# Attention of a transformer layer on one core: the order of the work rebuilt around pairs of heads and pairs of query tiles

## What is computed

```python
x = x + attn(layernorm(x))    # 16 heads, 64 plain + 64 rotated dims each, causal
x = x + ffn(layernorm(x))     # ternary weights: sign(W) * mean|W|, SiLU gate, 2048 wide
# attn, per head h:
scores = q[h] @ k[h].T * 128 ** -0.5          # causal, k from x, q from a latent of 256
out   += softmax(scores) @ (kv_lat @ Wv_up[h]) @ Wo[h]   # kv_lat: latent of 128
```

## Time and profile before

| | us |
|---|---|
| median of 3 runs | 2064.77 |
| lowest, highest | 2064.74, 2067.74 |
| the profiled execution | 2071.07 |
| its span, first to last instruction | 2069.3 |
| PE busy | 1929.1 (93%) |
| DVE busy | 1350.7 (65%) |
| ACT busy | 1060.1 (51%) |
| POOL busy | 526.0 (25%) |

### The profile page before, as it was taken

The page is one execution under the profiler, slowest core; times in us unless marked ns, Lnnn a source line. Parts: engine busy times, 40 slices in busy tenths (PEclk is TensorE's granted clock), DMA queues, the critical chain, the costliest instruction groups (busy, mean ns, idle before and its releaser), DMA issues. The chain is left out here.

```text
span 2069.3 us, 31835 instructions
## 1 busy us (share of the span) xinstructions
PE 1929.1 (93%) x11304; PEld 1668.5 (81%) x11304; DVE 1350.7 (65%) x2832; ACT 1060.1 (51%) x2531; POOL 526.0 (25%) x333
## 2 busy tenths in 40 slices
PE   6888875799999999999999999999999979999999
PEld 4666664699898898899899899889989968787877
DVE  5455554678778788788788688788778763333333
ACT  2233332567566566576566576576666652222222
POOL 6234343523222331331331322422412100000000
PEclk9998988899999999999999999999999989999999
DMA  3497988721120320320310301302202030000000
GB/s 109 137 232 206 228 203 215 205 62 27 53 62 1 78 62 1 79 60 3 78 38 26 78 15 48 78 1 62 68 11 62 1 123 1 21 0 20 0 20 20
DMA packets 67594, 144.61 MB, mean 70 GB/s; under 512 B 6880, under 2 KB 23520, under 8 KB 63328
## 3 DMA queue, kind: packets, MB, share of 16 engines
q1 hardware_dynamic: 67424, 142.50, 26.1%
HBM read 94.24 MB, written 48.23 MB: 69 GB/s over the span
## 5 line engine op out<-in xcount | busy, mean ns | idle before, releaser
L996 ACT CAST turned_hi<-ps_turn 128x512 fp32r<-128x512 f32 (+1 forms) x576 | 314.4, 566 | 377.2 <-PE ps_turn L1164 377.2
L1070 DVE TENSOR_TENSOR turned_lo<-ps_turn,turned_hi 128x512 fp32r<-128x512 f32 (+1 forms) x576 | 370.1, 659 | 129.1 <-ACT turned_hi L996 124.6
L969 ACT ACTIVATE probs<-ps_scores,bias 128x512 f32<-128x512 f32 (+3 forms) x642 | 401.6, 634 | 27.6 <-DVE bias L1063 12.9
L1164 PE MATMUL ps_turn<-ident,probs 128*128 128x128 f32 x2176 | 319.1, 275 | 0.8 <-ACT probs L969 0.2
L1134 PE MATMUL ps_scores<-k_hi,q_hi 128*128 128x512 f32 (+2 forms) x642 | 258.8, 403 | 37.0 <-issue 24.4
L1164 PEld LDWEIGHTS ps_turn<-ident,probs 128*128 128x128 f32 x2176 | 250.8, 140 | 27.1 <-ACT probs L969 3.0
L1037 DVE TENSOR_REDUCE negmax<-ps_scores 128x1 f32<-128x512 f32 x384 | 258.4, 681 | 3.5 <-PE ps_scores L1134 3.3
L1141 PE MATMUL ps_o<-turned_hi,kv_hi 128*128 128x256 f32 x1152 | 248.0, 297 | 6.2 <-DVEq L1069 6.1
L1134 PE MATMUL ps_scores<-k_lo,q_hi 128*128 128x512 f32 (+2 forms) x642 | 239.3, 373 | 0.0
L1134 PE MATMUL ps_scores<-k_hi,q_lo 128*128 128x512 f32 (+2 forms) x642 | 238.0, 371 | 0.0
L1141 PEld LDWEIGHTS ps_o<-turned_hi,kv_hi 128*128 128x128 f32 x1152 | 199.7, 190 | 44.4 <-issue 11.5
(11 more groups left out here) (156 smaller groups left out, 3495.6 us busy)
## 6 DMA issues: line engine op xcount, KB each, us to landing
rotT<-rot_out SPq DMA_DIRECT2D x64, 256.0 KB, 4.3
plainT<-plain_out SPq DMA_DIRECT2D x64, 256.0 KB, 5.1
k_raw<-plainT SPq DMA_DIRECT2D x16, 512.0 KB, 5.5
k_raw<-rotT SPq DMA_DIRECT2D x32, 256.0 KB, 6.6
q_raw<-plainT SPq DMA_DIRECT2D x16, 512.0 KB, 8.5
q_raw<-rotT SPq DMA_DIRECT2D x32, 256.0 KB, 9.0
all_signs<-signs SPq DMA_DIRECT2D x24, 256.0 KB, 4.8
signs_in<-all_signs SPq DMA_DIRECT2D x12, 512.0 KB, 8.7
```

The costliest lines, as they stand in the source:

```text
L969: nc.scalar.activation(probs[:, u % 2, t, first_key:first_key + keys], ps_scores[:, n % RING, 0:keys], ACT.Exp, scale=-1.0 if crosses(u, t ...
L996: nc.scalar.copy(turned_part(0, n, u, s), turned_psum(n, u, s)).then_inc(turned_hi_ready, 1)
L1070: nc.vector.tensor_tensor(turned_part(1, n, u, s), turned_psum(n, u, s), turned_part(0, n, u, s).bitcast(F32), ALU.subtract).then_inc(turn ...
L1164: last = nc.tensor.transpose(ps_turn[:, n % 2, at * P:(at + 1) * P], probs[:, u % 2, t, key:key + P], ident[:])
```

## The change

Only `attention` and its plan are rewritten. Both heads of a pair are worked on together: a tile of 128 queries has both heads' columns side by side.

- *Tiles and slots.* `SLOTS` pairs tile 15 with 0, 14 with 1, and so on to 8 with 7: 8 slots a pair, each with 9 steps and 10 pieces of scores over both heads. The first tile of a pair is thus the one with the most keys.
- *Steps.* A step is up to two key blocks of one tile, both heads: four transposes, or two where one block is left (`step_blocks`). No block above the diagonal is turned or multiplied: three value matmuls of 256 columns a block.
- *Two steps together.* `turn` of an even and the following odd step stand side by side in the plan, two steps ahead of their values; both banks of `ps_turn` are taken at once (`TURN_BANKS`), the turned halves have four places (`TURNED`). All values of a step wait for `turned_lo`.
- *Outputs.* Four a slot (two tiles, two heads), all in the second bank of `ps_o`, which also holds the values of the slot's second tile. Each waits for the add before it.
- *The plan.* `Plan` gives every event a time in steps (72 a pair) and sorts by it. Scores stand one slot ahead of the turns, across pairs: an event whose time falls before or after the pair's 72 steps belongs to the body of the pair before (`EARLY`) or after (`LATE`). Every pair's body is written out with those of its neighbours: one before the loop, 3 iterations of two pairs each, one behind it.
- *Loads.* k comes in four chunks of 512 tokens, both heads (`load_k`, 3 DMAs), q by slot (`load_q`, 6 DMAs of 128 tokens), wvo by head (`load_w`). `k_raw` and `q_raw` have two places each, `w_raw` one; each load waits until GpSimd has split what was there. The splits stay 18 a pair, each 512 columns.
- *Start.* No load is issued before the stores have left. Then the first pair's `EARLY` part runs: k chunks 0 and 1, wvo, k chunk 2, wvo, k chunk 3, q of slots 0 to 2, and behind them a sign chunk and `y`. VectorE waits for all of `y` between that part and the first pair's own.

TensorE's order by plan time in slot 1 (steps 9 to 17), from step 10: turn 3 and 4; scores; scores; out; scores; values 1; values 2; out; turn 5 and 6; out; values 3; scores; scores; out; values 4; scores; scores; turn 7 and the first of the second tile; values 5; values 6; scores; turn, turn; values 7; scores; values. In VectorE's order from the same turn: turned_lo 3, maximum, add, maximum, maximum, turned_lo 4, add, turned_lo 5, add, maximum, turned_lo 6, maximum, add, maximum, maximum, turned_lo 7, turned_lo. In ScalarE's: turned_hi 3, turned_hi 4, exp, split, exp, turned_hi 5, exp, turned_hi 6, exp, split, turned_hi 7, turned_hi, exp, exp, exp, exp, split, turned_hi, turned_hi.

The diff, cut to the plan, the loops of SP and VectorE, and TensorE's body:

```diff
--- before.py
+++ after.py
-QCH = 256
-TPU = QCH // P
-UPH = T // QCH
-UNITS = 2 * UPH
 PIECE = CH
 RING = 4
-SPLITS = 2 * NC + 1
-FIRST = 3
...
+TURN_BANKS = 2
+TURNED = 4
+RAW = 2
+SLOTS = tuple((NT - 1 - n, n) for n in range(NT // 2))
+NSLOTS = len(SLOTS)
+def npieces(t):
+    return -(-(t + 1) // TC)
+def piece(t, p):
+    return p * PIECE, min(PIECE, (t + 1) * P - p * PIECE)
+def nsteps(t):
+    return -(-(t + 1) // 2)
+def step_blocks(t, s):
+    return min(2, t + 1 - 2 * s)
+class Plan:
+    SCORES = {(4, 1): (0.5, 1.2, 1.6, 1.7, 3.8, 3.9, 4.6, 4.7, 6.7, 8.2),
+              (3, 2): (0.0, 0.8, 0.9, 1.5, 2.7, 3.6, 5.0, 5.2, 5.5, 6.7)}
+    def __init__(self):
+        self.events = []
+        lengths = [sum(nsteps(t) for t in tiles) for tiles in SLOTS]
+        begin = [sum(lengths[:n]) for n in range(NSLOTS)]
+        self.total = sum(lengths)
+        step = 0
+        for n, tiles in enumerate(SLOTS):
+            at = iter(self.SCORES[tuple(npieces(t) for t in tiles)])
+            for i, t in enumerate(tiles):
+                for h in range(2):
+                    for p in range(npieces(t)):
+                        x = begin[n] - lengths[n - 1] + next(at)
+                        self.put(x, "scores", n, i, h, p)
+                        self.put(x + 0.36, "maximum", n, i, h, p)
+                    for p in range(npieces(t)):
+                        self.put(x + 0.67 + 0.41 * p, "exp", n, i, h, p)
+            for i, t in enumerate(tiles):
+                for s in range(nsteps(t)):
+                    group, odd = step - step % 2, step % 2
+                    self.put(group - 2 + 0.01 * odd, "turn", n, i, s)
+                    self.put(group - 1.98 + 0.28 * odd, "turned_hi", n, i, s)
+                    self.put(group - 1.56 + 0.81 * odd, "turned_lo", n, i, s)
+                    x = group + (1.42 if odd else 0.8)
+                    self.put(x, "values", n, i, s)
+                    step += 1
+                self.put(x + 0.02, "o_hi", n, i)
+                self.put(x + 0.76, "o_lo", n, i)
+            for at, (i, h) in enumerate(((0, 0), (0, 1), (1, 0), (1, 1))):
+                self.put(x + 1.86 + 0.9 * at, "out", n, i, h)
+                self.put(x + 2.0 + 0.9 * at, "add", n, i, h)
+        for n in range(NSLOTS):
+            x = begin[n] - 18
+            self.put(x - 7, "load_q", n)
+            self.put(x + 2.6, "split_q", n)
+        for c, n in enumerate((1, 2, 4, 5)):
+            x = begin[n] - self.total
+            self.put(x - 7, "load_k", c)
+            for h in range(2):
+                self.put(x + 4.6 + 2 * h, "split_k", c, h)
+        x = begin[3] - self.total
+        for h in range(2):
+            self.put(x - 7 + 14 * h, "load_w", h)
+            self.put(x + 4.6 + 10 * h, "split_w", h)
+        for m in range(len(MATS)):
+            for part in range(3):
+                self.put(12 + 24 * m + 3.1 * part, "sign", m, part)
+            self.put(20 + 24 * m, "store_sign", m)
+        self.events.sort(key=lambda e: e[0])
...
+            sp.sem_inc(w_raw_free, 1)
             sp.dma_start(mask[:], hbm["mask"]).then_inc(mask_loaded, 16)
-            for n in (1, 0):
-                load_qk(sp, 0, 0, n, slice(CH, T), first_loaded[1])
-            load_chunk(sp, 0, 0)
+            body(-1, (EARLY,), back=1)
+            load_sign(sp, 0, 0)
             for m in range(NC):
                 rows = slice(TC * m, TC * (m + 1))
                 sp.dma_start(y[:, rows, :], hbm["x"].rearrange("(t p) d -> p t d", p=P)[:, rows, :]
                              ).then_inc(y_loaded[m], 16)
+            body(0, (OWN, EARLY))
+            done()
+            with sp.Fori(0, PAIRS // 2 - 1) as it:
                 for j in range(2):
-                    sp.wait_ge(raw_free, j + 1)
-                    following = sp.snap((i + 1) % PAIRS)
-                    load_head(sp, i if j == 0 else following, 1 - j)
-                    for m in SIGNS[j]:
-                        sp.wait_ge(signs_ready, m + 1)
-                        sp.dma_start(weight_chunks(hbm["signs"][m])[bass.ds(i, 1), :, :], signs[:]
-                                     ).then_inc(signs_stored, 16)
-                        load_chunk(sp, (m + 1) % len(MATS), i if m + 1 < len(MATS) else following)
-                sp.sem_inc(raw_free, -2)
-                sp.sem_inc(signs_ready, -len(MATS))
+                    body(sp.snap(2 * it + j + 1), (LATE, OWN, EARLY))
+                    done()
+            body(PAIRS - 1, (LATE, OWN))
+            sp.wait_ge(signs_stored, 16 * (1 + len(MATS)))
...
+            body((EARLY,), back=1)
+            for m in range(NC):
+                dve.wait_ge(y_loaded[m], 16)
+            body((OWN, EARLY))
+            done()
+            with dve.Fori(0, PAIRS // 2 - 1) as it:
+                for j in range(2):
+                    body((LATE, OWN, EARLY))
+                    done()
+            body((LATE, OWN))
+            done()
+            body((LATE,))
         @block.tensor
         def _(pe):
+            def body(par, following, back=0):
+                for f, kind, args in plan.of(following):
+                    j = (par + f) % 2
+                    if kind == "scores":
+                        n, i, h, p = args
+                        t = SLOTS[n][i]
+                        keys = piece(t, p)[1]
+                        if (i, h, p) == (0, 0, 0):
+                            if n == 0:
+                                pe.wait_ge(k_ready, k_splits.upto((NC - 1, 1), f - back))
+                            pe.wait_ge(q_ready, q_splits.upto((n,), f - back))
+                        pe.wait_ge(exp_done, softened.upto(args, f - back))
+                        wide = max(keys, 2 * P)
+                        for m, (x, z) in enumerate(parts(0, 1)):
+                            last = nc.tensor.matmul(ps_scores[:, pieces.number[args] % RING, 0:wide],
+                                                    q[n % 2][x][:, 2 * i + h, :],
+                                                    k_of(j, z, h, p)[:, 0:wide],
+                                                    start=(m == 0), stop=(m == 2))
+                        last.then_inc(scores_ready, 1)
+                    if kind == "turn":
+                        n, i, s = args
+                        t = SLOTS[n][i]
+                        at, bank = in_turn(*args)
+                        pe.wait_ge(exp_done, RING + softened.upto((n, i, 1, s // 2), f - back))
+                        pe.wait_ge(turned_lo_ready, lows.upto(args, f - back))
+                        for b in range(step_blocks(t, s)):
+                            key = (2 * s + b) * P
+                            for h in range(2):
+                                last = nc.tensor.transpose(ps_turn[:, bank, (2 * b + h) * P:(2 * b + h + 1) * P],
+                                                           probs_of(n, i)[:, h, key:key + P], ident[:])
+                        last.then_inc(turn_ready, 1)
+                    if kind == "values":
+                        n, i, s = args
+                        t = SLOTS[n][i]
+                        at, bank = in_turn(*args)
+                        blocks = step_blocks(t, s)
+                        if s == 0 and i == 0:
+                            pe.wait_ge(o_lo_ready, 2 + o_lows.upto(((n - 1) % NSLOTS, 0), f - back - (n == 0)))
+                        if s == 0 and i == 1:
+                            pe.wait_ge(out_added, 1 + outs.upto(((n - 1) % NSLOTS, 1, 1), f - back - (n == 0)))
+                        pe.wait_ge(turned_lo_ready, TURN_BANKS + lows.upto(args, f - back))
+                        for m, (x, z) in enumerate(parts(0, 1)):
+                            for b in range(blocks):
+                                last = nc.tensor.matmul(ps_o[:, i, 0:2 * P], kv[x][:, 2 * s + b, :],
+                                                        turned[z][:, at, 2 * P * b:2 * P * (b + 1)],
+                                                        start=(s == 0 and (m, b) == (0, 0)),
+                                                        stop=(s + 1 == nsteps(t) and (m, b) == (2, blocks - 1)))
+                        if s + 1 == nsteps(t):
+                            last.then_inc(o_ready, 1)
+                    if kind == "out":
+                        n, i, h = args
+                        if (n, i, h) == (0, 0, 0):
+                            pe.wait_ge(w_ready, w_splits.upto((1,), f - back))
+                        if (i, h) == (0, 0):
+                            pe.wait_ge(o_lo_ready, 2 + o_lows.upto((n, 1), f - back))
+                        pe.wait_ge(out_added, outs.upto(args, f - back))
+                        for m, (x, z) in enumerate(parts(0, 1)):
+                            last = nc.tensor.matmul(ps_out, o[x][:, i, h * P:(h + 1) * P], w[j][z][:, h, :],
+                                                    start=(m == 0), stop=(m == 2))
+                        last.then_inc(out_ready, 1)
```

(33 more changed lines are left out.)

615 lines of the change are left out of this document (255 added, 360 removed).

## The result

The changed kernel took 2084.89 us (median of 4 runs, 2083.91 to 2087.84), the one before 2064.76 us (median of 4): ratio 1.0101, 95% interval 1.0087 to 1.0115. Slower by 1.0%, 20 us. Forecast: 2089 us.

What follows compares the result with a forecast made beforehand. The prediction took TensorE's own work in the attention stage as the bound. To 2064.77 us it added -22.7 - 25.5 + 23 + 4 + 45 = +24, so 2089 us; range 2036 to 2122.

Steps and rivals of the forecast that it cites:

- values: Value matmuls on TensorE: 408 a pair instead of 432, as the zero blocks go; -22.7 us.
- loop ends: Jumps back in the attention stage: two instead of seven, 5.1 us each of idle time and slow clock; -25.5 us.
- loads: SP's transfers of q and k: 68 a pair instead of 20, issued far enough ahead to cost nothing.
- start: Start of the attention stage: first scores 17.3 us later, then a wait for y; +23 us, bounds +10 and +30.
- end: End of the attention stage: four last outputs share one bank, each after the add before it; +4 us.
- order in a pair: Engine orders inside a pair: short waits of 0.7 us a slot, 64 slots; +45 us (13 to 83).
- a wait of VectorE for y until about 409: Start of the stage: VectorE waits for all four y chunks, 4.5 MB at 222 GB/s, until 409.5.
- (a): Outputs stand closer in TensorE's order than output and add take; shortfalls of 1.6 us a pair.
- (b): Both turning banks taken at once, so the next turn waits for both turned_lo; three slots lose 0.7 to 1.7 us.
- Rival 1: Order inside a pair holds, TensorE stays full: 0 to 0.2 us a slot, likeliest 2048 us; chance 0.36.
- Rival 2: Pair borders still break, from long code and not the jump: five borders keep 5.1 us, 2114 us; chance 0.04.
- Rival 3: Short waits inside a pair cost TensorE clock: a tenth of each pair at 1.2 GHz, 2153 us; chance 0.05.

Runs made afterwards that it cites:

- E1: The kernel before, with the eight iterations of its attention loop written out and no jump: 2029.67 us, ratio 0.9829.
- E2: The changed kernel, with its three iterations of two pairs written out, so without the two jumps: 2079.09 us, ratio 1.0069.
- E8: The changed kernel, same instructions, with new plan times for the orders of all three engines: 2022.38 us, ratio 0.9792.
- E6: The changed kernel, with the second turned_lo of each two 0.36 steps earlier in VectorE's order: 2129.68 us, ratio 1.0317.
- E4: The changed kernel, where a slot begins on an odd step, its first turn 0.9 steps later, turned halves delayed too: 2101.44 us, ratio 1.0186.
- E5: The changed kernel, with a slot's outputs 1.22 steps apart instead of 0.9 and adds 0.4 behind them instead of 0.14: 2042.95 us, ratio 0.9896.
- E10: The changed kernel with E8's plan times, its jumps written out as in E2, and slot 6's outputs closer together: 2011.31 us, ratio 0.9746.
- E11: The changed kernel, with each step turned by itself and outputs 1.22 steps apart, adds 0.4 behind them: 2104.11 us, ratio 1.0189.
- E7: The changed kernel, with the loads of k's first two chunks issued before the wait for the last stores: 2084.4 us, ratio 1.0102.

## Why the prediction was right

The direction and size were right (slower, 2084.9 of 2089), by its own reasons for the most part. That the sum came within 4 us is in part luck: the start was put 9 us too high, the order and the end together some 7 us too low. Besides, the order's 45 us were a choice between 13 and 83 that no row could narrow.

| term | predicted | measured | from |
|---|---|---|---|
| values | -22.7 | about -23 | 3264 matmuls |
| loop ends | -25.5 | -26 to -28 | E1: 34.2; left: 8.0 by periods, 5.8 by E2 |
| loads | 0 | 0 | no wait of ScalarE for q or k inside a pair |
| start | +23 | about +14 | below |
| end | +4 | about +6 | below |
| order in a pair | +45 | about +50 | (9.6 - 3.3) x 8 |
| sum | +24 | +19 to +21 | medians: +20.1 |

*Loop ends.* Five jumps went, as said. The two that are left cost somewhat less than before, 2.7 to 4.0 us instead of 4.9; I had kept the old price, 5.1.

*Start.* The first score came at 381.50 instead of the forecast 385: 13.8 us later than in the earlier trace rows, or 15.6 counted from the last store of the stage before, which this execution issued 1.8 us sooner. The step that failed is "4.5 MB at the 222 GB/s of this stretch take until 409.5". The four y chunks were issued from 385.5 on and landed after 6.8 to 13.6 us, by 401; the window from then on moved 336 GB/s:

```profile
385.50:401.00 15.50, 10.11 (x45) 7.04 (x44) 6.51 (x16) 8.83 (x25) 1.28 (x1) 0.83 1.02 336
```

The 222 GB/s were no rate of a full queue. They are the mean of 40.5 us in which the DMA engines were busy 0.81 of the time, as the earlier trace rows shows. While they were busy all the time the kernel before moved 304 GB/s:

```profile
366.00:381.50 15.50, 8.86 (x30) 7.28 (x31) 5.21 (x16) 7.57 (x18) 7.36 (x6) 0.61 1.03 304
```

VectorE's first work behind that wait was released by turned_hi, not by y:

```profile
401.13 0.69 DVE L1083 TENSOR_TENSOR turned_lo<-ps_turn,turned_hi 128x512 fp32r<-128x512 f32 x1 [1.60 <-ACT turned_hi L1016]
```

So the 15 us of idle time behind the wait for y did not exist, and that sign of the prediction (a wait of VectorE for y until about 409) did not come. For what was lost behind the first score, the prediction's 11.7 us has a small misreading in it: its 5.2 us idle are a row of the weight loads, while TensorE itself was idle 6.5 us there, in several gaps (38.8 - 32.3). Counted in one way for both, from TensorE's starts and the prediction's prices over the 40 us behind the first score, 12.4 us were lost before and 11.7 now. 15.6 - 0.7 = 14.9, or 13.1 from the first score's own time: about 14, inside the bounds given.

*End.* From the end of the last values to the last add, less the matmuls in between, 8.0 us instead of 1.8. The chain is as described, each output behind the add before (timeline, TensorE), but from the second output on it ran at 1.2 GHz (starts 0.43 apart instead of 0.24), which I had left out:

```profile
1668.14 0.50 PE L1212 MATMUL ps_o<-wvo_hi,o_hi 128*128 128x512 f32 x1 [0.92 <-DVE o_lo L1089]
...
1675.45 0.79 PE L1212 MATMUL ps_o<-wvo_hi,o_hi 128*128 128x512 f32 x1 [1.24 <-DVE y L1103]
1676.05 0.63 PE L1212 MATMUL ps_o<-wvo_lo,o_hi 128*128 128x512 f32 x1
1676.47 0.63 PE L1212 MATMUL ps_o<-wvo_hi,o_lo 128*128 128x512 f32 x1
```

*Order inside a pair.* 158.9 - 149.3 = 9.6 us above TensorE's own work; the kernel before had 3.3. That is 0.78 us a slot more, 0.7 had been taken, and the bounds 0.2 to 1.3 were fair: E8 would lie below the lower one, E6 a little above the upper ((164.2 - 149.3 - 3.3) / 8 = 1.45). (a) was right in place and low in size, 2.5 us a pair before outputs (3.5 with the drawn-out slots) where 1.6 was the shortfall alone. (b) was right that orders, not loads, cost the time, and wrong in its cause. The waits for turned_lo are there, but half of what turns wait for (2.27 of 4.67 us a pair, steps 9 and 27) is the exponential, late behind VectorE's maxima; and the prediction saw in the adds only what they do to turned_lo and to the next output, not what they do to the maxima. E4 and E6 show that neither turn nor turned_lo was the lever, E5 that the place of the outputs and their adds was.

*Rivals.* Rival 1 (the order holds) fell for this list, with 0.78 us a slot where it wanted under 0.33; E8 shows that it was a matter of the list and not of the engines. Rival 2 fell with E1 and E2. Rival 3 fell: from 420 to 1570 us TensorE idled 34 us, all but the two loop ends in pieces of up to 1.2 us, and the granted clock of the window reads 1.00. The Trainium skill, TensorE: Matmul & The Clock Gate, section on psum-queue depth-cycling, tells of a kernel whose short idles made the clock swing; this trace does not show it. The Trainium skill's rule of strict order (same page, section on the architectural detail of Part 1) fits E6, where only VectorE's list was changed and 45 us were lost; no run tests it by itself.

## What to carry to other kernels

Where engines follow fixed lists, first write down for each chain through one buffer how long one turn of it takes, and place its members at least that far apart. Here an output at 1042.02 us and the next one, which had to wait for its add, at 1043.80 are 1.8 us apart. A list that is too tight makes an in-order engine wait, and the cost appears at whatever stands behind it, here an exponential and then a turn. Read a wait's releaser, then ask what made the releaser late; moving the waiting instruction (E4) or an earlier one in front of it (E6) moved the wait and made it longer. And look first for what is cheap: writing a loop of eight out, with the order as it was, gave 34 us, more than a rebuilt stage whose list was not fitted. Against that kernel (E1) even the fitted list without jumps (E10) gains 18 us (51.9 - 34.2), which is less than the 22.7 us of value matmuls that it saves.

## What the runs showed of the hardware that was not expected

- A jump back cost 4.9 us each in the kernel before, 3.5 of them idle, 2.7 to 4.0 with the changed kernel's list; eight times as long a straight code cost nothing to be seen (E1).
- A short wait of TensorE cost more than itself: the slot of 512 columns behind it took 0.33 us instead of 0.23. Over a pair this was 9.1 us instead of 7.75.
- Waits of up to 1.2 us, 28 us in 1150, left the granted clock at 1.00; the idle stretches of 2.6 to 3.5 us at the jumps were followed by 1.2 GHz.
- While y landed, 336 GB/s moved; the kernel before reached 304 where its DMA engines were as busy. The mean of a window in which they are not is no rate to plan with.
- The pattern of waits repeats from pair to pair to about 0.02 us in the changed kernel, in E2, E8 and E10, so that waits of 0.1 us can be assigned to single places of the list. It does not in E11, whose periods are 160.0 and 161.6.
- The first loads, issued 2.5 us sooner beside the last stores, were no sooner there: the first split began at 362.3 instead of 362.05 (E7).
